# Two-pick MoE combination: the second picks on ScalarE's queue and ScalarE, one VectorE addition for each chunk

## What is computed

```python
def _L1_ffn_ref(x, W_router, W1, b1, W2, b2):
    probs = jax.nn.softmax(x_flat @ W_router, axis=-1)
    topk_p, topk_i = jax.lax.top_k(probs, 2)
    topk_p = topk_p / topk_p.sum(axis=-1, keepdims=True)
    combine = (jax.nn.one_hot(topk_i, E) * topk_p[..., None]).sum(axis=1)
    for e in range(E):
        h = jax.nn.relu(x_flat @ W1[e] + b1[e])
        y = h @ W2[e] + b2[e]
        out = out + combine[:, e:e + 1] * y
    return out.reshape(B, T, C)
...
t = t + _L1_attn_ref(_ln_t(t), ...)
t = t + _L1_ffn_ref(_ln_t(t), ...)
```

## Time and profile before

| | us |
|---|---|
| median of 3 runs | 345.46 |
| lowest, highest run | 340.9, 346.23 |
| the profiled execution's own time | 341.68 |
| its span, first to last instruction | 339.8 |
| PE, DVE, ACT, POOL busy | 258.0, 185.8, 132.9, 104.8 |
| mean granted TensorE clock | 0.907 of full speed |

### The profile page before, as it was taken

How to read it: one execution, slowest core, us unless ns; L and a number is a source line. 1 busy time by engine, 2 the same in 40 slices (tenths; PEclk the granted TensorE clock), 3 DMA queues, 4 the chain that set the end, 5 groups by cost and what they waited for, 6 DMA issues and landing times.

```text
span 339.8 us, 6469 instructions
## 1 busy us (share of the span) xinstructions
PE 258.0 (76%) x2137; PEld 217.5 (64%) x2137; DVE 185.8 (55%) x690; ACT 132.9 (39%) x336; POOL 104.8 (31%) x109
## 2 busy tenths in 40 slices
PE   8799769776697766686866798786988589999700
PEld 7699557662665635555635677765877579989600
DVE  4555556473876865875865363474446422333136
ACT  8632322335344253344142236142535135646400
POOL 8202310111205206025141106323374534544500
PEclk9879999999989999999658799796999699999955
DMA  7999760500504307025007508416323565676066
GB/s 258 297 382 394 285 93 2 87 11 17 78 2 74 53 0 122 6 54 73 2 26 181 79 1 164 110 51 180 110 70 111 152 168 162 169 201 181 21 192 179
DMA packets 33377, 40.75 MB, mean 120 GB/s; under 512 B 3889, under 2 KB 21430, under 8 KB 33344
## 3 DMA queue, kind: packets, MB, share of 16 engines
q1 hardware_dynamic: 30784, 36.09, 41.5%
q0 software_dynamic: 2272, 4.22, 4.7%
q10 hardware_dynamic: 288, 0.02, 0.1%
HBM read 20.18 MB, written 14.17 MB: 101 GB/s over the span
## 4 chain that ended last, share of the span: by engine, by line
PE 40%; DVE 23%; DMA 18%; ACT 6%; issue 6%; SPq 4%; POOL 1%; DVEq 0%; POOLq 0%; ACTq 0%
DMA stack<-split 14%; PE bM L1084 8%; PE bS L1068 8%; PE bA L807 4%; DVE nm L1294 3%; PE bS L937 2%; ACT hT L795 2%; PE bL L1084 1%; PE bL L1054 1%; DVE t L1466 1%; DMA x_all<-xT 1%; SPq L526 1%; DMA rows_in<-lnx,slot 1%; DVE t L1470 1%; SPq L524 1%
## 5 line engine op out<-in xcount | busy, mean ns | idle before, releaser
L653 POOL DMA_INDIRECT rows_in<-lnx,slot x32 | 31.5, 986 | 69.7 <-DVE slot L1374 62.4
L795 ACT ACTIVATE hT<-bS,w1b 128x128 f32<-128x128 f32 x124 | 35.3, 370 | 35.2 <-PE bS L1068 35.2
L773 ACT ACTIVATE ec<-bE 128x512 f32<-128x512 f32 x48 | 27.5, 595 | 31.1 <-PE bE L972 18.5
L1084 PE MATMUL bM<-w2s,hT 128*128 x248 | 35.2, 287 | 4.8 <-ACT hT L795 2.4
L1084 PEld LDWEIGHTS bM<-w2s,hT 128*128 128x128 f32 x248 | 31.4, 198 | 7.2 <-issue 7.1
L1068 PE MATMUL bS<-xbT,w1b 128*128 128x128 f32 x248 | 34.5, 285 | 0.0
L807 PE MATMUL bA<-onesb 128*128 128x128 bf16 x408 | 31.4, 240 | 1.0 <-DVE onesb L1103 1.0
L1068 PEld LDWEIGHTS bS<-xbT,w1b 128*128 128x128 f32 x248 | 31.8, 201 | 0.2 <-issue 0.2
L807 PEld LDWEIGHTS bA<-onesb 128*128 128x128 bf16 x408 | 29.5, 110 | 3.5 <-issue 1.7
L1457 DVE TENSOR_TENSOR y<-bM,b2r 128x128 f32<-128x128 f32 x31 | 9.0, 292 | 37.0 <-PE bM L1084 36.7
L662 POOL DMA_INDIRECT rows_out<-y,goes x22 | 21.3, 970 | 23.7 <-DVE y L1457 21.9
(11 more groups left out here) (285 smaller groups left out, 564.6 us busy)
## 6 DMA issues: line engine op xcount, KB each, us to landing
w1b<-w SPq DMA_DIRECT2D x39, 258.0 KB, 3.6
rows_in<-hT SPq DMA_DIRECT2D x1, 8256.0 KB, 27.6
stack<-split SPq DMA_DIRECT2D x16, 256.0 KB, 5.7
xb<-rows_in SPq DMA_DIRECT2D x39, 64.5 KB, 2.3
w2s<-w SPq DMA_DIRECT2D x8, 256.0 KB, 6.2
stack<-split SPq DMA_DIRECT2D x16, 128.0 KB, 4.3
stack<-rows_out SPq DMA_DIRECT2D x8, 256.0 KB, 4.4
x_all<-xT SPq DMA_DIRECT2D x2, 512.0 KB, 4.7
```

What stands on the lines that cost most here:

```text
L653: pool.indirect_dma_start(out=rows_in, out_offset=bass.IndirectOffsetOnAxis(ap=slot[:, i, k, t:t + 1], axis=0), in_=lnx[:, i * TILES + t, ...
L773: act.activation(to, bE[u % 2][:, :], ACT.Exp).then_inc(at_e.sem, 1)
L795: last = act.activation(hT[:, b % 2, k, :], mo_banks(b)[1][:, k * P:(k + 1) * P], ACT.Relu, bias=w1b[:, b % W_RING, HID + k:HID + k + 1])
L1084: mm = pe.matmul(y_bank, hT[:, two, k, :], w2s[:, bass.ds(e, 1), k, :].rearrange("p a c -> p (a c)"), start=(k == 0), stop=(k == HB - 1))
```

## The change

One semaphore is saved in set-up: `su_stat` goes, and its count goes to `su_ones`. In the combination SP issues only the four loads of the first picks. ACT, when its tick list is done, waits for the `mo_out` semaphores too, issues the four loads of the second picks on its own queue, and then, for each chunk whose two loads have landed, gives four `activation` instructions Identity(w1 * back1 + 0), one for each tile, into `share`, a view of `ec0`; the last counts on the new `co_mul`. DVE keeps the four `scalar_tensor_tensor` of the first picks, then waits for the last of them and for the chunk's `co_mul`, and adds the whole chunk's products by one `tensor_tensor` of 128 x 512. `co_acc` counts chunks.

```diff
@@ -306,6 +306,7 @@
+        share = ec0[:, :, :].rearrange("p h (a n) -> p (h a) n", n=P)
@@ -417,7 +418,7 @@
-        co_one, co_acc, co_out = sig("co_one"), sig("co_acc"), sem("co_out")
+        co_one, co_mul, co_acc, co_out = sig("co_one"), sig("co_mul"), sig("co_acc"), sem("co_out")
@@ -578,13 +579,12 @@
             for n in range(ROWS_OUT):
                 sp.wait_ge(mo_out.sems[n], mo_out.total(n, BLOCKS))
             for c in range(IMAGES * TILES // CHUNK):
-                for k in range(PICKS):
-                    first = k * TOKENS + c * CHUNK * P
-                    sp.dma_start(back[:, c * CHUNK:(c + 1) * CHUNK, k, :],
-                                 rows_out[first:first + CHUNK * P, :].rearrange("(t p) c -> p t c", p=P))\
-                      .then_inc(co_in[c], 16)
+                first = c * CHUNK * P
+                sp.dma_start(back[:, c * CHUNK:(c + 1) * CHUNK, 0, :],
+                             rows_out[first:first + CHUNK * P, :].rearrange("(t p) c -> p t c", p=P))\
+                  .then_inc(co_in[c], 16)
             for c in range(IMAGES * TILES // CHUNK):
-                sp.wait_ge(co_acc.sem, co_acc.nth((c + 1) * CHUNK - 1))
+                sp.wait_ge(co_acc.sem, co_acc.nth(c))
@@ -797,6 +797,20 @@
             Ticks("act").run(at_part, l0_part, mo_part)
+
+            for n in range(ROWS_OUT):
+                act.wait_ge(mo_out.sems[n], mo_out.total(n, BLOCKS))
+            for c in range(IMAGES * TILES // CHUNK):
+                first = TOKENS + c * CHUNK * P
+                act.dma_start(back[:, c * CHUNK:(c + 1) * CHUNK, 1, :],
+                              rows_out[first:first + CHUNK * P, :].rearrange("(t p) c -> p t c", p=P))\
+                   .then_inc(co_in[c], 16)
+            act.wait_ge(at_tw.sem, at_tw.nth(LAST, 2))
+            for c in range(IMAGES * TILES // CHUNK):
+                act.wait_ge(co_in[c], 16 * PICKS)
+                for t in range(c * CHUNK, (c + 1) * CHUNK):
+                    last = act.activation(share[:, t, :], back[:, t, 1, :], ACT.Identity, scale=tw[:, t, 1:2], bias=none)
+                last.then_inc(co_mul.sem, 1)
@@ -1105,8 +1119,8 @@
-            last.then_inc(su_stat, 1)
-            dve.wait_ge(su_stat, 1)
+            last.then_inc(su_ones, 1)
+            dve.wait_ge(su_ones, 2)
@@ -1465,10 +1479,10 @@
                 for t in range(c * CHUNK, (c + 1) * CHUNK):
                     dve.scalar_tensor_tensor(out=t2[:, t, :], in0=back[:, t, 0, :], scalar=tw[:, t, 0:1], in1=t2[:, t, :],
                                              op0=ALU.mult, op1=ALU.add).then_inc(co_one.sem, 1)
-                for t in range(c * CHUNK, (c + 1) * CHUNK):
-                    dve.wait_ge(co_one.sem, co_one.nth(t))
-                    dve.scalar_tensor_tensor(out=t2[:, t, :], in0=back[:, t, 1, :], scalar=tw[:, t, 1:2], in1=t2[:, t, :],
-                                             op0=ALU.mult, op1=ALU.add).then_inc(co_acc.sem, 1)
+                dve.wait_ge(co_one.sem, co_one.nth((c + 1) * CHUNK - 1))
+                dve.wait_ge(co_mul.sem, co_mul.nth(c))
+                dve.tensor_tensor(t2[:, c * CHUNK:(c + 1) * CHUNK, :], t2[:, c * CHUNK:(c + 1) * CHUNK, :],
+                                  share[:, c * CHUNK:(c + 1) * CHUNK, :], ALU.add).then_inc(co_acc.sem, 1)
```

More of the change, by code:

```diff
@@ L377, in hybrid_block @@
         ld_x = [sem(f"ld_x{n}") for n in range(2)]
-        su_stack, su_zero, su_one, su_cast, su_dve, su_pe, su_act, su_pow, su_half, su_id, su_clear, su_stat, su_ones, su_last = (
+        su_stack, su_zero, su_one, su_cast, su_dve, su_pe, su_act, su_pow, su_half, su_id, su_clear, su_ones, su_last = (
             sem(n) for n in ("su_stack", "su_zero", "su_one", "su_cast", "su_dve", "su_pe", "su_act", "su_pow", "su_half",
-                             "su_id", "su_clear", "su_stat", "su_ones",
+                             "su_id", "su_clear", "su_ones",
                              "su_last"))
```

## The result

| | before | after |
|---|---|---|
| median of 6 runs, us | 341.92 | 343.34 |
| lowest, highest, us | 337.63, 346.23 | 340.73, 350.42 |
| ratio after / before, 95% interval | | 1.0142 (1.0083 to 1.0201) |
| span of the profiled execution, us | 339.8 | 341.3 |
| its granted TensorE clock | 0.907 | 0.906 |

By this first set the changed kernel is 1.4% slower, where I had forecast 0.3% faster. So the 1.4% rests on three executions on one side, and its interval ends at 2.01%.

The account below looks back on a forecast made before the run. The end was taken as first chunk's landing, DVE's 8.49 us without gap, and the last store (2.7). DVE's work -1.25, wait for ACT +0.5, earlier landing -0.4: 1.1 us less, 340.6 profiled, median 344.4; range 0 to 2.0 us less.

Parts of the forecast that it names:

- The whole time: Whole program: 1.1 us less, 340.6 us for the profiled execution and a median of 344.4; same 0.93, slower 0.03.
- How the numbers follow: Step to whole times: 1.1 us off 341.68 and off the median 345.46, as nothing changed touches what makes runs differ.
- Rival (d): Whole time: the change is too small to be seen, whatever its sign; said to be true of all cases.
- VectorE's work: Combination on DVE: 16 instructions replaced by four additions, 1.79 us a chunk against 2.12, 1.25 us less in all.
- ScalarE's price: ACT's added Identity activations of 128 x 128 from SBUF: 0.48 us each, 1.64 us for a chunk of four.
- Rival (a): ACT hidden: its four run in 1.2 us or less, like the ReLUs; 1.65 us less, 340.0; chance 0.15.
- The wait for ScalarE: First chunk: ACT's products come 0.5 us after DVE's four and DVE waits; in later chunks ACT is ahead.
- Rival (b): ACT sets the pace at 1.94 us a chunk, without overlap: about 0 to 0.4 us less, 341.5; chance 0.10.
- The first chunk: Loads on two queues: chunk 0 lands 0 to 0.7 us earlier, taken as 0.4.
- Rival (c): ScalarE's loads come late, chunk 0 landing at 330.2 instead of 328.6: 0.85 us slower, 342.5; chance 0.10.
- The later chunks: Loads of chunks 1 to 3 land ahead of DVE, with slacks of 0.3, 0.9 and 1.5 us, off the path.
- Sum inside the stage: Combination: 1.25 less for DVE's work, 0.5 back for waiting on ACT, 0.4 less for landing: 1.15 us less.

Follow-up runs that it names:

- isolated runs: Only the final combination, 16 times in a row, the rest of the program left out: 257.77 us as before the change, 243.78 us with the full change.
- iso_queue: Combination alone, 16 times, only the second picks' loads moved to ScalarE's queue, against the combination before: 250.59 us, 0.45 us less a repetition.
- iso_after: Combination alone, 16 times, with the full change, against the combination before: 243.78 us, 0.87 us less a repetition.

## Why the prediction was right or wrong

- **The whole time.** Predicted 0.3% faster, first measured 1.4% slower, then 1.0005 and 0.9994 in two further sets. The step that failed is in "How the numbers follow": it took the stage's 1.1 us off a median, with "nothing in the change touches what makes runs differ", and gave a slower result a chance of only 0.03. I had the spread of the runs (5.3 us for one program) but treated it as width alone. What the runs showed in its place: no lasting loss (two sets at 1.00, -0.3 us with an error of 0.3 at equal clock), and a spread which by itself moves such a ratio by more than the change. A single execution's time goes with its clock by 2.0 us for each 0.01, and in the first set three executions stood against five. The median itself moved too: 345.46 of three runs before, 341.92 of six. The measured 343.34 is near the forecast of 344.4 by luck, since a start 3.5 us too high and a step of the wrong sign stood against each other; the range of 339.0 to 346.3 held it by its width. "Within 2%" with 0.93 was right for the ratio itself; its interval ends at 1.0201. Rival (d), a change too small to be seen, is what the raw ratios show.
- **VectorE's work.** Predicted 1.79 us a chunk, 1.25 less in all; measured 1.78 in the trace, where the stretch less its landing and its wait fell from 8.49 to 7.15, which is 1.33. In the isolated runs the stretch less its landing and its waits of over 0.1 us fell from 8.56 to 7.15, which is 1.4. Right.
- **ScalarE's price.** Predicted 0.48 for one and 1.64 for four, measured 0.477 and 1.65. The Trainium skill's figure for ScalarE ("VectorE: DVE Perf Modes", section "The TRN2 errata"), which would have given 1.17, was contradicted by L741 beforehand and is contradicted by L812 now. Rival (a) fell: the width of an activation alone does not price it, the ReLU (L795, a bias operand, from PSUM) and the Identity (L812, a scale and a bias operand, from SBUF) of the same width take 0.37 and 0.48 us.
- **The wait for ScalarE.** Predicted 0.5 once; 0.67 once in the trace, 0.54 in the isolated runs plus 0.3 on average in later chunks. Mis-sized: I had the later chunks' data there ahead of ACT, but ACT waited for them in the isolated runs (mostly 0.15 to 0.6 us), and then DVE for ACT. Rival (b) fell: ACT's four overlap, 1.65 and not 1.94.
- **The first chunk.** Predicted 0.4 us sooner; 0.1 later in the trace (from 4.14 to 4.25 us after the issue), 0.06 (iso_queue) and 0.17 (iso_after) later in the isolated runs. The step that failed read the DMA share of 0.74 and 0.83 as work held up by late issues. With both halves issued at once the bytes began later instead (share 0.45 in the second us, not 0.74), and SP alone brought the first chunk in 3.75 to 4.14 us in three traces. The Trainium skill's rule ("DMA: Bandwidth & Descriptors", section "Issuing engines are not separate DMA queues"), by which a second issuing engine saves issue time only, was nearer for this term than my 0.4. The sum by it, 0.75, is nearer to 0.87 too, but only by chance: it has nothing for the queue, whose part measured 0.45. Rival (c), a landing over 4.8 us after the issue, did not occur in any of the whole-program traces (4.1 to 4.3 with two queues).
- **The later chunks.** Predicted to be there ahead of DVE with slacks of 0.3 to 1.5 us. I had read chunk 1's landing from the 4.0 of the earlier trace rows, which is the median of two loads. The fourth load by itself took 4.4 us (the view of line L583 for this load alone), so chunk 1 was there at 330.5 and its slack was 0.2:

```profile
L583 SPq DMA_DIRECT2D stack<-rows_out x1: 501/501/501, 326.2 to 326.2; - x1
...
DMA to landing us min/median/max: 4.4/4.4/4.4
```

The second trace of the same kernel has DVE waiting for chunk 1 by 0.84 us, and alone it waited by 0.48 on average. None of the five whole-program traces with two queues has such a wait of DVE. This cost was in the kernel before, unseen, and its removal is the queue's real gain of 0.45.
- **Sum inside the stage** (isolated runs): landing +0.17, work -1.41, waits for ScalarE +0.85, waits for chunk 1 -0.48: -0.87. I had -0.4, -1.25, +0.5 and nothing: -1.15. The total is near by luck: a loss missed and a gain missed stood against each other.

## What to carry to other kernels

Before a change of under 1% is judged by whole times, learn what one program against itself gives; here two sets of the same kernel had medians 3.3 us apart, and an edit worth 0.87 us could only be priced by running its stage alone, many times in a row. A slack of 0.2 or 0.3 us read from one trace is no slack, since the next execution can spend it. Where two engines meet in an addition, the half that lands first belongs to the engine with the longer way; exchanging the queues was worth 0.4 us more for no instruction.

## What was not expected of the hardware

- Time goes closely with the granted clock in a program with TensorE busy 76% of its span: 0.86 to 0.93 was granted from one execution to the next, 2.0 us for each 0.01.
- Two queues issuing at once did not start the bytes sooner: after 1.0 us of nothing, the DMA share was 0.45 in the second us, against 0.74 with one queue. Their first loads landed 3.5 us (SP) and 4.2 us (ACT) after the same moment, against 2.8 and 4.1 for SP's first two before.
- With eight loads on one queue, an issue behind the fourth took up to 2.5 us instead of 0.5, and the second chunk, issued on time, came late with it; with four on either queue it did not happen (longest issue 0.53 us alone behind the first repetition, 0.56 in the whole program).
